# Squares and folds on GpSimd, sums behind the minima, and a new order of score passes and of ScalarE's GELU turns

## The reference, cut to what matters

```python
q, k, v = (x @ Wq), (x @ Wk), (x @ Wv)        # 8 batches, 16 heads of 64
q = q * rsqrt(mean(q*q, -1) + eps) * q_rms_w  # the same for k: this is the sum of squares
gate = softplus(k . u_n / 8)
bias = -dist * omega * slope * gate           # and -inf above the diagonal
attn = softmax(q @ k.T / 8 + bias)
x = x + (attn @ v) @ Wproj + expert_ffn(x)    # 32 experts, GELU between two matmuls
```

## Time and profile before

| | us |
|---|---|
| median of 3 runs | 1347.58 (1347.16 to 1354.27) |
| the profiled execution | 1351.17, its span 1349.5 |
| TensorE busy | 1299.8 (96%) |
| VectorE busy | 1088.3 (81%) |
| ScalarE busy | 948.6 (70%) |
| GpSimd busy | 192.5 (14%) |

### The profile page before, as it was taken

One profiled execution on the slowest core, in us unless ns is written; L12 is line 12 of the kernel. 1 busy time (PEld: TensorE's weight loads), 2 busy tenths in 40 slices (PEclk: granted clock), 3 DMA queues, 4 the chain that ended last, 5 costly groups with the idle time before them and its releaser, 6 DMA issues. The chain is left out here.

```text
span 1349.5 us, 32126 instructions
## 1 busy us (share of the span) xinstructions
PE 1299.8 (96%) x11499; PEld 1092.0 (81%) x11499; DVE 1088.3 (81%) x3337; ACT 948.6 (70%) x2376; POOL 192.5 (14%) x565
## 2 busy tenths in 40 slices
PE   5899999999999999999999999999999799999999
PEld 3687788787977888797888878888887588888888
DVE  6869996999699779969996998799699867677663
ACT  5759885888588678859885888689588724444333
POOL 4512110111011111101111111111111100000000
PEclk8889999999999999999999999999999999999999
DMA  6452231332323222322332223233232321111100
GB/s 211 177 174 88 73 124 68 103 123 74 102 74 125 87 86 89 104 88 88 113 99 84 93 102 109 67 108 104 73 103 73 110 85 57 56 56 55 56 17 32
DMA packets 90830, 125.17 MB, mean 93 GB/s; under 512 B 8760, under 2 KB 77104, under 8 KB 90672
## 3 DMA queue, kind: packets, MB, share of 16 engines
q1 hardware_dynamic: 90352, 123.11, 28.4%
q10 hardware_dynamic: 320, 0.00, 0.0%
HBM read 103.69 MB, written 19.40 MB: 91 GB/s over the span
## 5 line engine op out<-in xcount | busy, mean ns | idle before, releaser
L1196 ACT ACTIVATE prob<-prob,low 128x512 f32<-128x512 f32 (+3 forms) x512 | 280.9, 551 | 119.2 <-DVE low L1352 119.2
L1352 DVE CUSTOM_DVE_ANT_0 prob<-at,mask 128x512 f32<-128x512 f32 (+3 forms) x512 | 219.8, 485 | 10.0 <-PE at L943 10.0
L930 PE MATMUL at<-w_hi,c_lo 128*128 128x386 f32 x512 | 188.0, 367 | 1.5 <-DVE area_raw L1297 1.5
L930 PE MATMUL at<-w_hi,c_hi 128*128 128x386 f32 x512 | 174.1, 340 | 0.0
L930 PE MATMUL at<-w_lo,c_hi 128*128 128x386 f32 x512 | 173.8, 339 | 0.0
L1365 DVE TENSOR_SCALAR prob<-prob,rec 128x512 f32<-128x512 f32 (+3 forms) x512 | 166.8, 389 | 4.5
L982 PE MATMUL at<-ident,prob 128*128 128x128 f32 x1280 | 164.2, 275 | 3.3 <-DVE low L1352 1.9
L1010 PE MATMUL at<-probT,v 128*32 128x512 f32 (+3 forms) x2048 | 151.1, 435 | 6.7 <-DVE probT L1375 3.7
L982 PEld LDWEIGHTS at<-ident,prob 128*128 128x128 f32 x1280 | 142.2, 140 | 10.7 <-DVE yT_lo L1381 1.6
L1010 PEld LDWEIGHTS at<-probT,v 128*32 128x32 f32 x2048 | 67.8, 109 | 90.8 <-issue 82.0
L1205 ACT ACTIVATE probT<-at 128x512 f32<-128x512 f32 (+1 forms) x256 | 130.6, 537 | 4.8 <-PE at L982 1.5
(11 more groups left out here) (255 smaller groups left out, 3186.6 us busy)
## 6 DMA issues: line engine op xcount, KB each, us to landing
area_w<-in_L_ffn_w SPq DMA_DIRECT2D x65, 1024.0 KB, 5.5
bias<-in_L_ffn_w SPq DMA_DIRECT2D x160, 32.0 KB, 4.4
x_in<-in_L_attn_x SPq DMA_DIRECT2D x8, 512.0 KB, 5.9
xr<-in_L_attn_x SPq DMA_DIRECT2D x8, 512.0 KB, 4.7
eo_d<-hidT SPq DMA_DIRECT2D x32, 128.0 KB, 1.8
x_d<-xr SPq DMA_DIRECT2D x8, 512.0 KB, 2.9
area_raw<-x_d SPq DMA_DIRECT2D x8, 512.0 KB, 4.0
out<-area_raw SPq DMA_DIRECT2D x7, 512.0 KB, 3.1
```

Of the source, the lines that this page charges most:

```text
L930: m = eng.matmul(bQ[n % 2][:, 0:W], a[:, (j // HP) % 2, k, n * P:(n + 1) * P], w[:, k, j % HP, :], start=start, stop=(k == KC - 1 and a is ...
L1196: eng.activation(sl, sl, ACT.Exp, scale=-1.0, bias=low[:, i:i + 1], accum_out=den[:, i:i + 1]).then_inc(exp_done.sem, 1)
L1352: eng.tensor_tensor_reduce(out=prob[s % 2][h][:, off[c]:off[c + 1]], in0=bC[i][:, at:at + (c + 1) * P], in1=mask[:, (NT - 1 - c) * P:T], s ...
```

## The change

`square` moves from ScalarE to GpSimd, as a multiplication of `raw` by itself. Behind it GpSimd runs a new step, `fold`, which adds the upper half of each head's 64 squares to the lower half and then the upper quarter to the lower, so that `mean_square` on VectorE sums 16 elements a head. `mean_square(s+1)` moves behind all eight minima of the turn. The pass of scores with `kT_lo` becomes the last of the four, that with `kaug` the third. In GELU turns ScalarE does `exps(s, 0)` behind `copy_k` and `take_raw(s+2, 2)` behind `copy_aug`.

```diff
--- before.py
+++ after.py
@@ -777,6 +777,7 @@
         w1n_load, w2n_load, small_load = ev("w1n_load", 2, 16), ev("w2n_load", 1, 16), ev("small_load", 5, 16)
         aug_done, v_done = ev("aug_done", 6), ev("v_done", 1)
         tok_done = ev("tok_done", 1)
+        folded = ev("folded", 2)
 
         pe_prep = ev("pe_prep", 1)
         prep_hi, prep_done, spread_set, prepared = ev("prep_hi", 1), ev("prep_done", 1), ev("spread_set", 5), ev("prepared", 1)
@@ -933,16 +934,16 @@
                     m.then_inc(pe_q.sem, 1)
 
                 def scores(s, c):
-                    for q, k, ready in ((qT_hi, kT_hi, k_hi_done), (qT_lo, kT_hi, q_lo_done), (qT_hi, kT_lo, k_lo_done),
-                                        (qaug, kaug, kaug_done)):
+                    for q, k, ready in ((qT_hi, kT_hi, k_hi_done), (qT_lo, kT_hi, q_lo_done), (qaug, kaug, kaug_done),
+                                        (qT_hi, kT_lo, k_lo_done)):
                         if c == NT - 1:
                             eng.wait_ge(ready.sem, ready.at(s))
                         for h in range(2):
                             i, at = place[c, h]
                             rows = slice(h * D, (h + 1) * D)
                             m = eng.matmul(bC[i][:, at:at + (c + 1) * P], q[rows, c * P:(c + 1) * P], k[rows, 0:(c + 1) * P],
-                                           start=ready is k_hi_done, stop=q is qaug)
-                            if q is qaug:
+                                           start=ready is k_hi_done, stop=k is kT_lo)
+                            if k is kT_lo:
                                 m.then_inc(pe_s.sem, 1)
 
                 def all_scores(s):
@@ -1152,13 +1153,6 @@
                         eng.wait_ge(gate_in.sem, gate_in.at(j - 2))
                     eng.activation(raw[:, j % 2, n, :], bQ[n % 2][:, 0:W], ACT.Copy).then_inc(raw_A.sem, 1)
 
-                def square(j):
-                    eng.wait_ge(raw_A.sem, raw_A.at(j))
-                    eng.wait_ge(raw_D.sem, raw_D.at(j))
-                    eng.wait_ge(ssd.sem, ssd.at(j - 1, 1))
-                    eng.wait_ge(pe_t.sem, pe_t.at(j - 1, 2))
-                    eng.activation(sq[:, :, :], raw[:, j % 2, :, 0:2 * P], ACT.Square).then_inc(squared.sem, 1)
-
                 def rsqrt(j):
                     eng.wait_ge(ssd.sem, ssd.at(j))
                     eng.activation(lnv[:, :], ss[:, :], ACT.Ln).then_inc(r0_done.sem, 1)
@@ -1226,7 +1220,6 @@
                     if (b, i) == (B - 1, 0):
                         take_raw(0, 2)
                         take_raw(0, 3)
-                        square(0)
                     if (b, i) == (B - 1, 2):
                         rsqrt(0)
                     if (b, i) == (B - 1, 3):
@@ -1241,8 +1234,6 @@
                 take_raw(1, 2)
                 take_raw(1, 3)
                 for s in range(NTURN + 1):
-                    if s + 1 < NTURN:
-                        square(s + 1)
                     if s % 4 == 2:
                         gelu(s // 4)
                     elif s < NTURN:
@@ -1268,10 +1259,10 @@
                         exps(s, 2)
                     if s + 1 < NTURN and s % 4 != 2:
                         gate(s + 1)
-                    if s + 2 < NTURN:
+                    if s + 2 < NTURN and s % 4 != 2:
                         take_raw(s + 2, 2)
                     prepare(s, 2)
-                    if s < NTURN:
+                    if s < NTURN and s % 4 != 2:
                         exps(s, 0)
                     if s > 0:
                         copy_y(s - 1)
@@ -1282,7 +1273,12 @@
                     if s + 1 < NTURN:
                         copy_q(s + 1)
                         copy_k(s + 1)
+                    if s % 4 == 2:
+                        exps(s, 0)
+                    if s + 1 < NTURN:
                         copy_aug(s + 1)
+                    if s + 2 < NTURN and s % 4 == 2:
+                        take_raw(s + 2, 2)
                     if s + 2 < NTURN:
                         take_raw(s + 2, 3)
                     prepare(s, 3)
@@ -1297,8 +1293,8 @@
                     eng.tensor_copy(raw[:, j % 2, 0, :], bQ[0][:, 0:W]).then_inc(raw_D.sem, 1)
 
                 def mean_square(j):
-                    eng.wait_ge(squared.sem, squared.at(j))
-                    eng.tensor_reduce(ss[:, :], sq[:, :, :].rearrange("p n (i d) -> p (n i) d", d=D), AX.X,
+                    eng.wait_ge(folded.sem, folded.at(j))
+                    eng.tensor_reduce(ss[:, :], sq[:, :, :].rearrange("p n (i d) -> p (n i) d", d=D)[:, :, 0:D // 4], AX.X,
                                       ALU.add).then_inc(ssd.sem, 1)
                     eng.wait_ge(ssd.sem, ssd.at(j, 1))
                     eng.tensor_scalar(ss[:, :], ss[:, :], 1.0 / D, EPS, ALU.mult, ALU.add).then_inc(ssd.sem, 1)
@@ -1433,11 +1429,10 @@
                     if s < NTURN:
                         lows(s, 3)
                         lows(s, 1)
+                        lows(s, 2)
+                        lows(s, 0)
                     if s + 1 < NTURN:
                         mean_square(s + 1)
-                    if s < NTURN:
-                        lows(s, 2)
-                        lows(s, 0)
                     if s + 2 < NTURN:
                         take_raw(s + 2)
                     prepare(s, 0)
@@ -1495,6 +1490,20 @@
                     eng.tensor_tensor(ag[:, :, 3:AG:D], shift32[:, :, :], ag[:, :, 2:AG:D].bitcast(F32),
                                       ALU.subtract).then_inc(aug_done.sem, 1)
 
+                def square(j):
+                    eng.wait_ge(raw_A.sem, raw_A.at(j))
+                    eng.wait_ge(raw_D.sem, raw_D.at(j))
+                    eng.wait_ge(ssd.sem, ssd.at(j - 1, 1))
+                    eng.wait_ge(pe_t.sem, pe_t.at(j - 1, 2))
+                    eng.tensor_tensor(sq[:, :, :], raw[:, j % 2, :, 0:2 * P], raw[:, j % 2, :, 0:2 * P], ALU.mult).then_inc(squared.sem, 1)
+
+                def fold(j):
+                    eng.wait_ge(squared.sem, squared.at(j))
+                    of_head = sq[:, :, :].rearrange("p n (i d) -> p (n i) d", d=D)
+                    eng.tensor_tensor(of_head[:, :, 0:D // 2], of_head[:, :, 0:D // 2], of_head[:, :, D // 2:D], ALU.add).then_inc(folded.sem, 1)
+                    eng.wait_ge(folded.sem, folded.at(j, 1))
+                    eng.tensor_tensor(of_head[:, :, 0:D // 4], of_head[:, :, 0:D // 4], of_head[:, :, D // 4:D // 2], ALU.add).then_inc(folded.sem, 1)
+
                 def take_v(j):
                     eng.wait_ge(raw_A.sem, raw_A.at(j))
                     eng.wait_ge(raw_D.sem, raw_D.at(j))
@@ -1506,6 +1515,8 @@
                     eng.tensor_copy(tok[:, :, 0:B], merged[:, :, m, :]).then_inc(tok_done.sem, 1)
 
                 route.gpsimd(eng)
+                square(0)
+                fold(0)
                 route.over(eng)
                 augment(0)
                 take_v(0)
@@ -1513,6 +1524,8 @@
                     if begins_in(s) is not None:
                         take_tokens(begins_in(s))
                     if s + 1 < NTURN:
+                        square(s + 1)
+                        fold(s + 1)
                         augment(s + 1)
                         take_v(s + 1)
                     if s in (1, 2):
```

## The result

The changed kernel takes **1491.38 us** (median of 4 runs, 1487.52 to 1496.56), the kernel before 1350.92 in the same comparison: a ratio of 1.104 [1.098, 1.110]. The prediction was slower, 1432 us in a range of 1385 to 1485. The direction was right, but the time is 59 us above the forecast and 6 above the range. The profiled execution took 1487.52 us (span 1485.7), 136.35 more than the one of before. Executions of one kernel differ by some 10 us, which goes with TensorE's granted clock in the stage ahead of the first turn, so profiled executions are also compared from the first turn on: there the changed kernel is 139.5 us longer.

The account below looks back on a forecast made before the run. TensorE, 96% busy, was taken to bound the kernel. Ordinary turns 57.6, behind outputs -2.5, GELU turns 22.4, behind them 5.3 and start 1.5 made +84 on 1351.17, so 1435, as a median 1432 us; range 1385 to 1485.

Parts of the forecast that it names:

- The meeting: Start of a turn: GpSimd's square and first fold hold VectorE's `divide` at shared ports, first minimum 2.9 us later.
- Ordinary turns: 24 turns with s%4 of 0 or 1, each 2.4 us longer through the late minimum: 57.6 us.
- 0.35 was counted on at `values`: TensorE's wait for VectorE's last `copy_p` ahead of `values`: 0.35 us a turn gained back by VectorE's shorter sum.
- The clock: TensorE's clock in the turns: no loss entered in the sum, falling to half left to rival 3.
- rival 3: TensorE's clock halves in the new 2.5 us waits: +34 us in half of 40 turns, +68 in all; 11%.
- Behind a GELU turn: 15 turns: square starts behind `divide`, so no meeting; later sum and `copy_aug` cost 0.35 us each, 5.3 in all.
- GELU turns: 16 turns: meeting delays ScalarE's exponentials, the new order gives part back; each grows by 1.4 us, 22.4 in all.
- behind outputs: 7 turns behind a batch's outputs: VectorE's delay lies under TensorE's output matmuls, `values` gains 0.35 each: -2.5 us.
- The start: Ahead of the first turn: `mean_square(0)` waits for square and folds, between 0 and 2.4 us, taken as +1.5.
- Rival 1: GpSimd doesn't hold VectorE up at the shared ports; turns gain, 1324 us in all; chance 7%.
- rival 2: GpSimd's square waits until all four pieces of `divide` are through; `values` slightly late, 1358 us in all; chance 6%.
- The order of the passes: Scores on TensorE: taking `kT_lo` last spares at most 0.17 us, hidden where the minimum is late: 0.

Follow-up runs that it names:

- Run 1: The changed kernel, with GpSimd's square made to wait until the four pieces of `divide` at the start of the turn are done: 1367.9 us.
- run 2: The changed kernel, with 11 projections (5 behind a GELU turn) added to fill TensorE's wait in most turns, their results overwritten: 1456.81 us.
- run 5: The changed kernel with the square back on ScalarE; folds on GpSimd, short sum and both new orders kept: 1332.46 us.
- run 4: The kernel before with only the two changes of order (pass with `kT_lo` last, ScalarE's order in GELU turns): 1341.1 us.
- run 3: The changed kernel without the two folds; GpSimd only squares, VectorE sums 64 elements a head behind all minima: 1432.91 us.
- run 6: The kernel before with only the square moved from ScalarE to GpSimd; sums and orders as before: 1440.13 us.
- run 7: The changed kernel with both orders put back as before; square and folds on GpSimd, sum behind the minima: 1523.82 us.

## Why the prediction was right or wrong

**The meeting: right, in order and nearly in size.** The square comes between the first piece of `divide` and the second, the third passes, the first fold comes between the third and the fourth. Forecast was a first minimum at 4.5 into the turn, measured 4.26: the square starts earlier and is shorter (it ends 2.73 into the turn where 3.05 was taken), the first fold is longer (1.44 for 1.2). Run 1 shows it as the cause, since the same work without the meeting costs 16 us instead of 140. Nothing in the program makes a piece of `divide` wait for the square, so the two engines meet in another place than at a semaphore. The Trainium skill, "SBUF — State Buffer", section "Who interferes with whom", states both halves of what the runs show: the hold by whoever came first, and the freedom of a VectorE instruction with one input in SBUF, outside the two-port modes. For the first the trace has 1919 ns instead of 281; for the second, which no row of before could show, the minimum beside the square in run 1, 0.69 as ever.

**Ordinary turns: right but for the clock,** with some luck. Forecast +2.4; at full clock (run 2) 16.3 - 14.0 = +2.3. Two small errors cancel in this. The transposes start 2.36 later (5.10 for 2.74) and run 0.1 longer, 2.5 in all where the sum had 2.7; but only 0.2 of that comes back, where 0.35 was counted on at `values`. In run 5, without a hold, 0.27 comes back. The sum also counted 24 such turns; 23 grew, since turn 0 has no `divide` at its start.

**The clock: the step that failed.** The sum took it at nothing, and rival 3, "TensorE's clock falls in the new waits", got 11%. It fell in 27 turns, at 1.3 us each: 27 x 1.3 = 35 us, and run 2 measured 35. The rival's own price, "in half of them, +34", came so close by luck: it had 20 turns at 1.7, where 27 at 1.3 were measured. The argument against it was that in the turns before, the clock had not fallen "with waits of 0.45 at most". That reading of the trace is wrong. The first row below, from the waits of the turns between 220 and 1150 us, has a longest wait of 1.6, at full clock; the others show TensorE's longest wait in the routing stage after its first 13 us, 1.81, and two stretches with the columns of the earlier trace rows, the one in which that wait lies and the next:
```profile
PE at L1010 <- DVE probT L1375: 3.5, 6, 1.6
...
21.05 0.39 PE L364 MATMUL at<-c_lo,gT_hi 128*32 128x512 f32 x1 [1.81 <-DVE c_lo L573]
...
18.32:21.73 3.41, 1.59 (x11) 1.01 (x10) 2.91 (x8) 3.41 (x8) 2.97 (x7) 1.00 0.83 335
21.73:25.15 3.42, 3.42 (x15) 2.28 (x14) 3.20 (x12) 2.71 (x6) 2.73 (x6) 0.50 0.55 187
```
The clock is at half from 21.73 on, 0.7 behind the end of that wait. This does not show the wait to be the reason, since the clock of that stage also fell at 79.76, behind a stretch in which TensorE was busy without a break; but with waits of 1.6 at full clock and one of 1.81 ahead of half clock, a wait of 2.5 deserved far more than 11%. Its 34 us then belong in the sum, or at the least well inside the range. The Trainium skill, "TensorE: Matmul & The Clock Gate", Part 1, says that idleness drops the clock to half; the trace agrees (0.51 for 3.41 us, behind a wait of 2.31).

**Behind a GELU turn: "no meeting" was wrong.** I took the square to start at 1.9 into the turn, behind `divide`. The timelines of ScalarE, GpSimd and VectorE in the turn from 481.22, and the single line of the fourth piece:
```profile
481.90 0.86 ACT L1154 ACTIVATE area_raw<-at 128x386 f32<-128x386 f32 x2
...
482.84 1.91 POOL L1498 TENSOR_TENSOR area_sq<-area_raw 128x1024 f32<-128x1024 f32 x1 [3.64 <-ACT area_raw L1154]
484.82 1.28 POOL L1503 TENSOR_TENSOR area_sq<-area_sq 128x512 f32<-128x512 f32 x1
...
482.04 2.78 DVE L1361 TENSOR_SCALAR prob<-prob,rec 128x384 f32<-128x384 f32 x4
...
482.90 1.92 DVE L1361 TENSOR_SCALAR prob<-prob,rec 128x128 f32<-128x128 f32 x1
484.75 0.68 DVE L1348 CUSTOM_DVE_ANT_0 prob<-at,mask 128x512 f32<-128x512 f32 x1
```
The square started at 1.62, 0.06 ahead of the fourth piece, which took 1.92. The first minimum came at 3.5, where before it was 2.1, and the turn grew by 1.27 instead of 0.35: 15 x 0.92 = 14 us. An estimate of 1.9 with an error of 0.3 had been set against a `divide` that ends at 2.0; it could not exclude a meeting.

**GELU turns: sized too small.** Forecast +1.4, measured +1.92 at full clock: 8 us over 16. I had ScalarE's chain, which the new order shortens, set the end of the turn. But its length with the late minimum is TensorE's own work and wait, 14.17 + 2.31 = 16.48; the window of run 4 (14.04 busy of 14.04) shows that TensorE already sets it once the order is changed, so the whole delay counts: 16.49 - 14.04 = 2.45, less the 0.5 that the order gives.

**The sum, corrected.** Ordinary 23 x 2.3 = 53, GELU 16 x 1.92 = 31, behind them 14 x 1.27 = 18 (turn 3 hardly grew), behind outputs nothing (forecast -2.5): 102 us, as run 2 has from the first turn on. With 35 for the clock it is 137, and 2 more stand behind the start of the last turn, which has a stretch of low clock too: 139, measured 139.5. The start is -3.3 (forecast +1.5), but that tests nothing, since the routing stage had 13.7 us less of half clock in this execution than in the one of before; what the change costs there stays open. The clock is the largest error, 35 of the 59 us. The measured time lies only 6 above the range, though, so the 14 behind GELU turns or the 8 in them, sized right, would also have brought the sum into it.

**The forecast as a whole.** Rival 1 (no hold) and rival 2 (GpSimd waits for all four pieces) are excluded by the 1919 ns. The order of the passes is worth 0 in ordinary turns, as forecast (run 4).

## What to carry to other kernels

Before an operation is moved to GpSimd, lay its start over VectorE's timeline: beside VectorE's `tensor_scalar`s on SBUF data the square cost VectorE nearly its whole length, and each further GpSimd operation that was ready between two pieces cost its own once more. A fold of 1.28 us cost nothing when it started 0.06 behind them, and a square of 2 us cost 85 us over the kernel when it started 0.1 behind the start of the first. Where a change opens a wait on TensorE longer than any that the trace has at full clock, put a price on the clock in the sum, and not only on the wait; look up the longest such wait first. When two kernels differ by ten microseconds, see how far the clock of a stage where little was changed accounts for it. And when a change has several parts, run the parts: here the orders and the short sum were worth 19 us together, hidden under a loss of 160.

## What the runs showed of the hardware that was not expected

- The clock. Waits of 1.1 to 1.5 us ahead of the transposes (runs 3 and 6) never lowered it; waits of 2.3 or more did in 27 of 39 turns of the changed kernel (in none of the 8 of class 2, in all 8 of class 4), and there are 29 stretches in run 7. In the turns the low stretch lasts 3.4 us each time and costs 1.3. With the wait filled (run 2) it never came. Why some turns with the same wait escape it was not tested.
- The clock in the routing stage. The profiled executions have 10.2 us of half clock there (first turn at 82.8 to 83.9), 23.9 to 30.7 (87.2 to 89.8) or 44.4 (95.3 and 95.4), so a spread of 12.6 us stands ahead of the turns. What decides it was not tested.
- The turn-taking at the port. GpSimd gets in between two pieces of VectorE that follow on each other directly (0.08 of overlap), and then one piece of VectorE gets through ahead of GpSimd's next operation, which is ready 0.08 behind its last. In the turns where they meet at the start, the changed kernel has the pattern square, piece, fold, piece. Which piece the square holds goes with its start: the second in most turns, where it starts 0.12 behind the start of the first; behind GELU turns the fourth in the changed kernel, the third in run 3 and the first in runs 6 and 7. The held piece takes 1.9 to 2.1 us each time, whatever its size.
- An operation of GpSimd is stretched little itself: the fold of 512 elements takes 1.28 when it meets no piece and 1.44 in the meeting, the square 1.90 and 2.05, while VectorE's piece goes from 281 to 1919 ns.
